# Digits read and counted at the head of each turn, one ring of one-hots for each block half, transposed weights in two places

## What is computed

```python
h = relu(layernorm(x))
Wh = h @ W.T + b_W
e = leaky_relu((Wh @ a_src)[src] + (Wh @ a_dst)[dst] + a_b, 0.2)
attn = softmax of e over the edges of each target        # segment_max, exp, segment_sum
h_prime = segment_sum(attn * Wh[src], dst) + h @ res_W.T + res_b
x = x + gru(h_prime, h)
h = relu(layernorm(x))
for _ in range(4):
    msg = (h @ W_edge[type].T + b_edge[type])[src]       # type = argmax(edge_attr_4)
    h = gru(segment_sum(msg, dst), h)
return x + h
```

## Time and profile before

| | us |
|---|---|
| median of 3 runs | 498.57 (496.58 to 499.31) |
| the profiled execution | 496.89 |
| its span, first to last instruction | 495.1 |
| TensorE busy | 419.9 (85%) |
| VectorE busy | 289.2 (58%) |
| ScalarE busy | 173.4 (35%) |

### The profile page before, as it was taken

How to read it: one execution, slowest core, us unless ns; L and a number is a source line. 1 busy time by engine, 2 the same in 40 slices (tenths; PEclk the granted TensorE clock), 3 DMA queues, 4 the chain that set the end, 5 groups by cost and what they waited for, 6 DMA issues and landing times.

```text
span 495.1 us, 7979 instructions
## 1 busy us (share of the span) xinstructions
PE 419.9 (85%) x2536; PEld 289.4 (58%) x2536; DVE 289.2 (58%) x746; ACT 173.4 (35%) x310; POOL 12.0 (2%) x33
## 2 busy tenths in 40 slices
PE   1387686788777896777889999999999999999994
PEld 0375354477767795664336486464864647746484
DVE  6979789998898884554543445244462434533142
ACT  3620334666666665434322122021230212302021
POOL 2101000000000000101000000000000000000000
PEclk9879987999898899899999999999999999999999
DMA  6100000000000000000000000000000000000001
GB/s 163 25 1 0 1 1 1 1 1 2 1 2 2 2 2 1 0 0 1 1 5 1 0 1 1 1 0 1 0 1 0 1 0 3 0 1 0 23 0 32
DMA packets 5829, 3.48 MB, mean 7 GB/s; under 512 B 495, under 2 KB 5632, under 8 KB 5788
## 3 DMA queue, kind: packets, MB, share of 16 engines
q1 hardware_dynamic: 4516, 2.42, 1.9%
q10 hardware_dynamic: 1272, 0.54, 0.4%
HBM read 2.31 MB, written 0.64 MB: 6 GB/s over the span
## 4 chain that ended last, share of the span: by engine, by line
PE 65%; DVE 18%; issue 6%; ACT 6%; DVEq 4%; DMA 0%; POOL 0%; SPq 0%; ACTq 0%; POOLq 0%
PE small L1437 33%; PE big L1422 7%; DVE cell_hot L843 5%; PE small L1307 4%; PE big L1290 3%; DVE absent L864 3%; DVE absent L860 3%; DVEq L843 2%; PE big L1385 1%; PE big L1387 1%; PE big L1386 1%; PE big L1376 1%; PE big L1377 1%; PE big L1378 1%; ACT absent L461 1%
## 5 line engine op out<-in xcount | busy, mean ns | idle before, releaser
L1437 PE MATMUL small<-nibbles,store 128*128 128x512 fp8e4 (+1 forms) x960 | 174.1, 339 | 0.3 <-issue 0.3
L1437 PEld LDWEIGHTS small<-nibbles,store 128*128 128x128 f16 x960 | 93.5, 98 | 80.4 <-issue 8.8
L843 DVE TENSOR_SCALAR cell_hot<-iota,cell_w,fields 128x320 bf16<-128x320 f16 x264 | 75.0, 358 | 13.3 <-issue 8.8
L1290 PE MATMUL big<-cell_hot,store 128*128 128x320 bf16 x264 | 57.7, 345 | 25.3 <-DVE cell_hot L843 20.0
L1004 DVE TENSOR_TENSOR digit_words<-big,edge_rows 128x512 f32<-128x512 f32 x40 | 27.5, 691 | 65.4 <-PE big L1422 65.4
L610 ACT CAST store<-digit_words 128x512 f16<-128x512 f32 x40 | 24.6, 618 | 103.5 <-DVE digit_words L1004 103.5
L1290 PEld LDWEIGHTS big<-cell_hot,store 128*128 x264 | 35.6, 145 | 42.7 <-issue 38.0
L1422 PE MATMUL big<-wT,h 128*128 128x512 f32 x80 | 38.2, 597 | 3.1 <-ACT h L606 3.1
L1091 DVE TENSOR_SCALAR aS<-small,edge_down 128x256 f32<-128x256 f32 (+1 forms) x20 | 8.8, 474 | 39.7 <-PE small L1437 39.7
L947 DVE SCALAR_TENSOR_TENSOR cell_hot<-rz,cell_hot 128x256 f32<-128x256 f32 (+1 forms) x25 | 10.4, 418 | 35.5 <-ACT cell_hot L581 35.5
L1008 DVE TENSOR_TENSOR store<-digit_words,store 128x512 f16<-128x512 f32 x40 | 27.4, 687 | 4.5 <-ACT store L610 3.0
(11 more groups left out here) (241 smaller groups left out, 513.6 us busy)
## 6 DMA issues: line engine op xcount, KB each, us to landing
xn<-in_x SPq DMA_DIRECT2D x1, 576.0 KB
out<-xn SPq DMA_DIRECT2D x4, 128.0 KB
store<-in_edge_attr SPq DMA_DIRECT2D x1, 256.0 KB
wn<-in_L_gnn_W_edge SPq DMA_DIRECT2D x1, 256.0 KB, 6.5
wn<-in_L_gnn_Wi ACTq DMA_DIRECT2D x1, 192.0 KB, 3.9
wn<-in_L_gnn_Wh_g ACTq DMA_DIRECT2D x1, 192.0 KB, 6.2
wn<-in_L_gnn_W_ih SPq DMA_DIRECT2D x1, 192.0 KB, 6.2
wn<-in_L_gnn_W_hh SPq DMA_DIRECT2D x1, 192.0 KB, 6.2
```

The lines of the kernel that those rows point to most:

```text
L843: last = v.tensor_scalar(half_hot[:, b * GROUP + q], iota[:, b * HALF:(b + 1) * HALF], cell_w[:, half, bass.ds(tile + q, 1)], fields[:, 1, ...
L1290: last = mm(big[:, 2 * half + b, 0:HALF], lane_hot[:, :, bass.ds(tile + q, 1)].rearrange("p l a -> p (l a)"), half_hot[:, b * GROUP + q], ...
L1437: last = mm(bank[:, 0:w], m16[s % 2][:, i, part, t * P:(t + 1) * P], A8[:, t % 2, i, lo:lo + w, t // 2], start=(i == 0 and part == 0 and t ...
```

## The change

- VectorE's turn J becomes: digits of block J-1, one-hots of window 2J, cells, reciprocal of J-4, weigh J-2, table reads, one-hots of window 2J+1, cells, row maximum of J-1.
- TensorE's turn J becomes: count of J-1, window 2J, window 2J+1, transposes of J-2, aggregate of J-3.
- ScalarE's turn keeps the eviction of the second half of J-1 first; then come the copy of the transposed weights, the exponentials, the attention of J-4, absences and counts of J-1, the eviction of the first half of J, and the excesses.
- Each half has a ring of eight one-hots of its own: half 0 in `half_hot`, half 1 in the storage of `h1`, with semaphores of its own (`slot_a`, `pair_a`, `slot_b`, `pair_b`).
- The transposed weights go to `hn` for even blocks and to `probT` for odd ones, so the copy waits for the aggregate two blocks back. The second normalisation, which writes `hn`, waits for the aggregate of block 8, and the first residual waits for the eviction of the last block's first half.

```diff
+        half_hots = (half_hot, h1[:].bitcast(BF16).rearrange("p (u c) -> p u c", u=RING))
...
+        def probs_place(n):
+            return hn[:].rearrange("p i d -> p (i d)") if isinstance(n, int) and n % 2 == 0 else probT[:]
...
-                if later(n):
+                if not isinstance(n, int):
                     act.wait_ge(K.agg, n)
-                a.copy(probT[:], smallf[:, 0:NP]).then_inc(K.probsb, 1)
+                elif n >= 2:
+                    act.wait_ge(K.agg, n - 1)
+                a.copy(probs_place(n), smallf[:, 0:NP]).then_inc(K.probsb, 1)
...
             def window_cells(j, half):
                 if j >= 2:
-                    dve.wait_ge(K.pair, ends[j - 2])
+                    dve.wait_ge((K.pair_a, K.pair_b)[half], ends[j - 2])
...
-                            dve.wait_ge(K.slot, before + b * GROUP + u + 2)
+                            dve.wait_ge(slot, before + b * GROUP + u + 2)
...
             def turn(J):
+                if there(J - 1):
+                    read_digits(J - 1)
                 if there(J):
                     one_hots(2 * J, 0, ranges[2 * J])
-                if there(J - 1):
-                    read_digits(J - 1)
                 if there(J + 1):
                     window_cells(2 * J + 2, 0)
+                if there(J - 4):
+                    reciprocals(J - 4)
                 if there(J - 2):
                     weigh(J - 2)
                 next_range(2 * J + 1)
                 next_range(2 * J + 2)
                 if there(J):
                     one_hots(2 * J + 1, 1, ranges[2 * J + 1])
+                if there(J + 1):
+                    window_cells(2 * J + 3, 1)
                 if there(J - 1):
                     row_max(J - 1, J - 1)
-                if there(J + 1):
-                    window_cells(2 * J + 3, 1)
-                if there(J - 3):
-                    reciprocals(J - 3)
...
             def turn(J):
+                if there(J - 1):
+                    count_turn(J - 1)
                 if there(J):
                     next_window(2 * J, 0)
                 if J == 0:
                     score_rows()
-                if there(J - 1):
-                    count_turn(J - 1)
-                if there(J - 3):
-                    aggregate(J - 3)
                 if there(J):
                     next_window(2 * J + 1, 1)
                 if there(J - 2):
                     prob_turn(J - 2, min(J, NT))
+                if there(J - 3):
+                    aggregate(J - 3)
...
+            pe.wait_ge(K.evac, NW - 1)
             residual(0, 2)
```

More of the change, by code:

```diff
@@ L247, in build @@
         E1 = sems("e_", "sq link bound scale bias wide w_T w_sb spread rows_ps rows")
-        K = sems("k_", "cellw taken pair slot window evac digits countT absent counted excess rowmax logit "
+        K = sems("k_", "cellw taken pair_a pair_b slot_a slot_b window evac digits countT absent counted excess rowmax logit "
                  "lmax shift bent exps probs probT probsb agg denom recip attn")
@@ L497, in turn @@
                     probs_out(J - 3)
+                if there(J - 2):
+                    exponentials(J - 2)
                 if there(J - 4):
                     attn_out(J - 4, J - 4)
-                if there(J - 2):
-                    exponentials(J - 2)
+                if there(J - 1):
+                    absences(J - 1)
+                    counts_out(J - 1, count_sum[:, J - 1:J])
                 if there(J):
@@ L833, in one_hots @@
                 first, second, tiles, ahead = tiles_of
+                slot, pair = ((K.slot_a, K.pair_a), (K.slot_b, K.pair_b))[half]
                 dve.wait_ge(K.cellw, j + 1)
@@ L840, in one_hots @@
                         for u in range(0, GROUP, 2):
-                            dve.wait_ge(K.slot, before + b * GROUP + u + 2)
+                            dve.wait_ge(slot, before + b * GROUP + u + 2)
                             for q in (u, u + 1):
-                                last = v.tensor_scalar(half_hot[:, b * GROUP + q], iota[:, b * HALF:(b + 1) * HALF],
+                                last = v.tensor_scalar(half_hots[half][:, b * GROUP + q], iota[:, b * HALF:(b + 1) * HALF],
                                                        cell_w[:, half, bass.ds(tile + q, 1)],
@@ L846, in one_hots @@
                                                        ALU.is_equal, ALU.mult)
-                            last.then_inc(K.pair, 2)
+                            last.then_inc(pair, 2)
             def read_digits(n):
@@ L905, in turn @@
                     one_hots(2 * J + 1, 1, ranges[2 * J + 1])
+                if there(J + 1):
+                    window_cells(2 * J + 3, 1)
                 if there(J - 1):
                     row_max(J - 1, J - 1)
[L908 to L911 removed]
             dve.wait_ge(S0.table, 1)
[L914 removed]
+            ranges, ends = {}, {-2: 0, -1: 0}
             next_range(0)
@@ L1287, in window @@
                         for u in range(0, GROUP, 2):
-                            pe.wait_ge(K.pair, before + b * GROUP + u + 2)
+                            pe.wait_ge(pair, before + b * GROUP + u + 2)
                             for q in (u, u + 1):
@@ L1291, in window @@
                                           lane_hot[:, :, bass.ds(tile + q, 1)].rearrange("p l a -> p (l a)"),
-                                          half_hot[:, b * GROUP + q], start=False, stop=False, skip_group_check=True)
-                            last.then_inc(K.slot, 2)
+                                          half_hots[half][:, b * GROUP + q], start=False, stop=False, skip_group_check=True)
+                            last.then_inc(slot, 2)
                 for b in range(2):
@@ L1323, in aggregate @@
                 for i in range(NT):
-                    last = mm(psD[:, 0:P + 1], probT[:, i * P:(i + 1) * P], Wh[:, i], start=(i == 0),
+                    last = mm(psD[:, 0:P + 1], probs_place(n)[:, i * P:(i + 1) * P], Wh[:, i], start=(i == 0),
                               stop=(i == NT - 1), skip_group_check=True)
@@ L1337, in edge_biases @@
                 mm(psD, ones[:], spread.rearrange("p t o -> p (t o)"), start=True, stop=True).then_inc(E1.rows_ps, 1)
-            ahead = [0]
+            ahead = [0, 0]
             def next_window(j, half):
-                tiles_of, ahead[0] = edge_tiles(pe, j, ahead[0])
+                tiles_of, ahead[half] = edge_tiles(pe, j, ahead[half])
                 window(j, half, tiles_of)
             def turn(J):
+                if there(J - 1):
+                    count_turn(J - 1)
                 if there(J):
@@ L1361, in _ @@
             pe.wait_ge(S0.w_sb, 4)
-            pe.sem_inc(K.slot, RING)
+            pe.sem_inc(K.slot_a, RING)
+            pe.sem_inc(K.slot_b, RING)
             for J in range(NT):
```

6 lines of the change are left out of this document (3 added, 3 removed).

## The result

| | before | changed |
|---|---|---|
| median, us | 498.5 (496.58 to 499.31) | 507.85 (507.38 to 508.15) |
| profiled execution, us | 496.89, span 495.1 | 508.09, span 506.3 |
| ratio of the times | 1 | 1.0197, 95% interval 1.0177 to 1.0217 |

An execution more than 1.5% above the fastest of its kernel is left out of the ratios; of all runs here that is one, of the tenth experiment. By the trace it does both things that the forecast spoke of: turns 4 to 9 are shorter, and turns 1 to 3 and the end lose more than that.

A forecast was written before the change was run, and what follows sets the result against it. VectorE was taken as the bound of the turns touched. Costs 2.8 + 5.9 + 1.6 + 0.6 less a gain of 4.1 made +6.8, 503.7 against the profiled execution, given as 504.5 us; range 498 to 509.5.

The forecast's parts named there:

- Turns 4 to 9: VectorE's later turns: no row maximum waits, a turn takes 11.96 us; gain 4.1, bounds 3 to 8.5.
- The chosen piece: VectorE, reciprocal to second one-hot loop: reads start 0.15 us after the reciprocal; 2.53, of which 0.88 is idle.
- Turns 1 and 2: Early turns with digits and count ahead of 16 one-hots: cost 2.8 us in turn 1 and 5.9 in turn 2.
- The late eviction: Turn 2: VectorE's digits wait 3.2 us for ScalarE's eviction of window 3, behind the scaling of the edge weights.
- The half level: TensorE's clock at 1.2 GHz for the count after idling; VectorE's ring stall taken as 2.5 us in turn 1, 3.0 in turn 2.
- The full level's 0.7: Turn 1: VectorE's ring stall if TensorE counts at 2.4 GHz, 0.7 us, against 3.0 at the half level.
- Turn 3: Cost 1.6 us (1.0 to 3.3): a turn of 15.6 against 13.96, with a ring stall of 1.3.
- The end: TensorE's aggregate of block 6 moves behind window 19, making block 9's count later only by part: 0.6 us (0 to 2.4).
- Edits costed at nothing: Copies to two places and new waits on aggregates cost nothing; separate rings save nothing, slot waits being only 0.44 us.
- Reads that stay covered: Rival: VectorE's sequencer passes the reciprocal, saving 6.3 us together: 497.4, no change; chance 0.17.
- Digits that wait for the eviction: Rival: VectorE's digits wait for the second half's eviction in every turn, about 1 us each: 509; chance 0.10.
- Row maxima that still wait: Rival: VectorE's row maximum still waits for `absent`, losing 4.9 us of the gain: 508.6; chance 0.03.

The follow-up runs named there:

- the tenth experiment: Changed kernel with one place for the transposed weights, so each copy waits for the aggregate of the block ahead: 516.05 us, ratio 1.0379.
- the ninth experiment: Changed kernel with VectorE's weigh moved ahead of denominator and reciprocal, so the reciprocal stands right ahead of the table reads: 514.86 us, ratio 1.0331.
- the fourth experiment: Changed kernel with one of each turn's two table reads moved into the row maximum of the turn ahead: 501.73 us, ratio 1.0087.
- The fifth experiment: Changed kernel with old VectorE and TensorE order in turns 1 to 3, and aggregate 6 ahead of window 19 again: 495.35 us, ratio 0.9955.
- the eighth kernel: Changed kernel, old order in turns 1 to 3, aggregate 6 ahead of window 19, first reads earlier, later one read inside the row maximum: 491.49 us, ratio 0.9886.

## Why the prediction was right, and where its sum was short

The forecast of 504.5 was 3.4 below the median, within its range and on the right side. Its sum against the profiled execution was +6.8 where the traces have +11.2. The mechanisms were the forecast's; the terms that were too small are the stall of turn 3 and the end.

**Turns 4 to 9** (4.1 forecast, 4.4 found). Each step held: no row maximum waits, a turn is 11.84 to 12.28 (11.96 forecast), 0.75 to 1.26 is idle ahead of the second loop. The chosen piece, reads that start behind the reciprocal, is what the ninth experiment shows: moved, the reciprocal takes the reads along. By the Trainium skill, page "Perfetto Trace Analysis", section Sequencer Loop, an instruction is pushed into a queue and waits there, so the reads should pass it. Before the change the reads did pass instructions whose waits were met: they began at 110.9, ahead of the cells at 111.50 and weigh at 111.65. A reciprocal that still waits is not passed: behind it they begin at 124.1 and it at 123.94, and in the ninth experiment at 123.4 and it at 123.36. The measurement decides for this kernel. In its source the wait is a statement of its own ahead of the reciprocal, and whether the sequencer stands in that or in the reciprocal the trace doesn't tell. The step was incomplete in one point: the cells' wait holds the sequencer as well, which puts the same idle into turns 2 and 3, where the forecast had counted it inside the reads.

**Turns 1 and 2** (8.7 forecast, 8.8 found). The late eviction is 3.17 (3.2), the stalls are 3.21 and 2.35 (2.5 and 3.0). That the sums agree to 0.1 is luck: the two stalls missed by 0.7 either way, and over the five traces of this order the stall of turn 1 goes from 2.16 to 3.22. The half level, which I chose, was there, and it came from TensorE's idle time, as argued: with zeros in that time the stalls are 1.28 and 1.27. The full level's 0.7 was too small, though. In turn 1 the digits now cover a loop head that had left 0.7 idle ahead of window 2's one-hots, which pays for the reads. The kernel with the count late and the one with both orders old show that these waits are real losses and not covers for something else.

**Turn 3** (1.6 forecast, 2.8 found). The term that was too small is the stall, put at 1.3 because "TensorE has just worked": TensorE then idled 2.49 for the digits and ScalarE's copy, the count took 3.51 at a granted clock of 0.66, and the stall was 2.42. But that idle time does not always bring the half level. In the fourth experiment the count behind the same 2.49 took 2.39:

```profile
104.06 2.39 PE L1322 MATMUL small<-ident,nibbles 128*128 128x128 f16 x40 [2.49 <-ACT hn L492]
```

The stall there is 1.36, and 1.38 in the ninth, the same again: the forecast's 1.3. Which of the two the other executions of the changed kernel had is not known.

**The end** (0.6 forecast, 2.6 found). "Later only by part" was a guess where the rows allowed a sum: the aggregate costs about 2.25 on TensorE, window 19 closes 0.7 earlier for it (1.2 behind the start of row maximum 8 instead of 1.9), which leaves 1.6. The fifth experiment gives that back. The other 0.9 goes with aggregate 8, which took 3.67 in the profiled execution against 2.40 before, 1.3 more, of which the idle time behind it gives 0.5 back (1.17 against 1.64); no run takes that by itself.

**Edits costed at nothing.** The rings are worth nothing in the old order; what they are worth in the new one no run takes, and none takes ScalarE's new order by itself. No wait of the trace is put down to the second place, but the forecast never asked what it is worth: without it this order loses some 8 to 9 us more. Had the diff lacked it, the time would have lain outside the range.

**The rivals.** Reads that stay covered: refuted here, but the eighth kernel, with a read moved, comes near what that rival had for the later turns (8.1 of 8.5). Digits that wait for the eviction: absent in the changed kernel from turn 4 on; with turns 0.9 shorter they are there in two turns of the fourth experiment and once in the eighth. Row maxima that still wait: none. The 1.1 ahead of turn 1 is in nobody's sum; in the kernels that change nothing ahead of the first cells, those start anywhere from 48.87 to 50.44.

## What to carry to other kernels

A new order that pays in the steady state can cost more in the first turns, where loops are longer than their ring and one-time work stands in other queues; cost those turns by themselves, and give them another order if need be. When a consumer's place in a queue moves, ask what it lets fill up meanwhile, and at which clock level it will run after the wait that it now has. An instruction that waits for its neighbour also held up the table reads and loop heads behind it here, so put those behind something long whose waits are met.

## What the runs showed of the hardware

- One table read with its register work takes some 0.86 us of VectorE's sequencer (one moved: idle of 2.50 became 1.64), a loop head 0.45 to 0.7 (the idle at 108.50 and 61.72 before the change); they run beside an instruction in progress, but not past one that still waits.
- Products of zeros ahead of the counts of turns 1 and 2 (2.33 and 4.77 us of them) brought these from 4.45 and 3.79 to 2.41 us. Idle time does not always bring the half level: behind the same 2.49 of it, one count took 3.51 and others 2.39.
- Without the second place the executions of one kernel lie 8 us apart (511.54 to 519.42), and those of the changed kernel 0.8. But those with a read moved lie 4.7 apart (500.13 to 504.84) with the second place in; why is open.
